# A two-layer recurrence on one core: layer 0's third state tile goes through TensorE in bfloat16 parts, and TensorE's loop body is cut at another place

## The reference

```python
def layer(x, h0, Wx, Wh, b):
    xW = jnp.einsum('ntd,dh->nth', x, Wx) + b
    def step(h_prev, xw_t):
        h_next = jnp.tanh(h_prev @ Wh + xw_t)
        return (h_next, h_next)
    _, hs = jax.lax.scan(step, h0, jnp.swapaxes(xW, 0, 1))
    return jnp.swapaxes(hs, 0, 1)
x = x + layer(x, cond, Wx0, Wh0, b0)
x = x + layer(x, cond, Wx1, Wh1, b1)
```

## Time and profile before

| | us |
|---|---|
| median of the runs | 2057.52 |
| the profiled execution's own time | 2059.2 |
| its span | 2057.4 |
| TensorE busy (matmul) | 2046.2 (99%) |
| VectorE busy | 1837.9 (89%) |
| ScalarE busy | 1539.9 (75%) |
| GpSimd busy | 444.0 (22%) |

### The profile page before, as it was taken

One profiled execution on the slowest core, in us unless ns is written; L12 is line 12 of the kernel. 1 busy time (PEld: TensorE's weight loads), 2 busy tenths in 40 slices (PEclk: granted clock), 3 DMA queues, 4 the chain that ended last, 5 costly groups with the idle time before them and its releaser, 6 DMA issues.

```text
span 2057.4 us, 224159 instructions
## 1 busy us (share of the span) xinstructions
PE 2046.2 (99%) x98384; PEld 1952.7 (95%) x98384; DVE 1837.9 (89%) x12254; ACT 1539.9 (75%) x7426; POOL 444.0 (22%) x2054
## 2 busy tenths in 40 slices
PE   8999999999999999999999999999999999999999
PEld 7999999999999999999999999999999999999998
DVE  5999999999999999999999999999999999999997
ACT  5777777777777777777777777777777777777776
POOL 3222222222222222222222222222222222222221
PEclk9999999999999999999999999999999999999999
DMA  3000000000000000000000000000000000000000
GB/s 106 28 24 28 24 27 25 26 25 26 26 25 26 25 27 24 28 24 28 24 28 24 28 24 28 24 28 24 28 24 28 24 28 24 28 24 27 25 26 18
DMA packets 111995, 56.59 MB, mean 28 GB/s; under 512 B 12432, under 2 KB 111008, under 8 KB 111520
## 3 DMA queue, kind: packets, MB, share of 16 engines
q1 hardware_dynamic: 111168, 53.53, 9.0%
q10 hardware_dynamic: 576, 1.18, 0.2%
q0 software_dynamic: 32, 0.02, 0.0%
HBM read 37.90 MB, written 16.78 MB: 27 GB/s over the span
## 4 chain that ended last, share of the span: by engine, by line
PE 99%; DMA 1%; issue 0%; DVE 0%; ACT 0%; ACTq 0%; SPq 0%
PE ps_rec L303 44%; PE ps_rec L324 33%; PE ps_xw L279 22%; DMA wx<-wx_in 0%; DMA wh<-wh_in 0%; PE ps_rec L376 0%; DVE zt L541 0%; ACT h L445 0%; SPq L255 0%; ACTq L498 0%; ACTq L497 0%; DVE x_out L581 0%; DVE z L550 0%; SPq L254 0%
## 5 line engine op out<-in xcount | busy, mean ns | idle before, releaser
L303 PE MATMUL ps_rec<-wh,h 128*32 128x128 f32 x33024 | 1271.8, 273 | 4.1 <-ACT h L445 2.7
L445 ACT ACTIVATE h<-z 128x16 f32<-128x16 f32 x4066 | 709.2, 217 | 481.7 <-DVE z L550 475.4
L324 PE MATMUL ps_rec<-wh_part,h 128*32 128x128 bf16 x48792 | 1047.4, 219 | 1.5 <-issue 1.5
L303 PEld LDWEIGHTS ps_rec<-wh,h 128*32 128x32 f32 x33024 | 832.5, 109 | 79.6 <-ACT h L445 9.2
L324 PEld LDWEIGHTS ps_rec<-wh_part,h 128*32 128x32 bf16 x48792 | 890.1, 97 | 15.4 <-issue 1.9
L541 DVE STREAM_TRANSPOSE zt<-ps_rec 128x64 f32<-128x64 f32 x4096 | 778.8, 228 | 94.0 <-PE ps_rec L303 14.2
L214 POOL TENSOR_TENSOR h<-h 128x16 f32<-128x16 f32 x2032 | 430.1, 212 | 1589.4 <-DVE h L214 1589.4
L434 ACT ACTIVATE ps_rec<-xw,mask 128x128 f32<-128x128 f32 x2040 | 731.9, 359 | 9.5 <-issue 1.0
L550 DVE TENSOR_REDUCE z<-zt 128x16 f32<-128x48 f32 x4066 | 650.6, 199 | 0.9
L214 DVE TENSOR_TENSOR h<-h 128x16 f32<-128x16 f32 x2034 | 357.3, 176 | 110.7 <-ACT h L445 2.8
L279 PE MATMUL ps_xw<-wx,x_pe 128*32 128x128 f32 x8248 | 409.9, 273 | 0.5 <-issue 0.5
(11 more groups left out here) (23 smaller groups left out, 22.3 us busy)
## 6 DMA issues: line engine op xcount, KB each, us to landing
x_pe<-x_t SPq DMA_DIRECT2D x256, 64.0 KB, 1.9
x_dve<-x_t SPq DMA_DIRECT2D x256, 64.0 KB, 2.0
out_t<-x_out SPq DMA_DIRECT2D x256, 64.0 KB, 1.7
wh<-wh_in SPq DMA_DIRECT2D x1, 1024.0 KB, 5.2
wx<-wx_in SPq DMA_DIRECT2D x1, 1024.0 KB, 8.2
wx<-wx_in ACTq DMA_DIRECT2D x1, 512.0 KB, 5.0
wx<-wx_in SPq DMA_DIRECT2D x1, 512.0 KB, 4.8
wh<-wh_in SPq DMA_DIRECT2D x1, 512.0 KB, 7.9
```

The source lines that it names most:

```text
L303: mm = pe.matmul(rows(ps_rec[l][n % 2], g), h_step(l, n - 1)[:, k, :], wh[l][:, k, g * P:(g + 1) * P], start=False, stop=k == KC - 1 and n ...
L324: mm = pe.matmul(ps_rec[l][n % 2][32 * g:32 * g + 32, cols], h_bits(l, n - 1)[:, k, :], wh_part[l][:, i, to + cols.start:to + cols.stop], ...
L445: act.activation(h_of(l, n)[:, tiles, :], src[:, tiles, :], ACT.Tanh).then_inc(h_count(l, n)[0], 1)
```

## The change

1. `KB = (3, 2)` and the table `PART_COLS`: layer 0's tile 2 goes in parts too. Its whole tiles are now only tile 3, its parts 36 matmuls and no longer 24.
2. The rests are dealt out anew. VectorE makes for layer 0 the first rest of tiles 0 and 1, then the first rest of tile 2 (which waits for the second tanh), then the second rest of tiles 0 and 1. GpSimd makes the second rest of layer 0's tile 2, and both rests of layer 1. The VectorE order of a slot has layer 0's three rests between `sum_out` and layer 1's `turn`.
3. Projected tiles go two at a time, both behind layer 0's parts; the one that stood between layer 1's parts and layer 0's whole tiles is gone from there.
4. TensorE's slot is cut in `head` (layer 0's parts, projection) and `tail` (layer 1, layer 0's next whole tiles), and the loop body begins with `tail`. All pieces of the weights, now five sets, are awaited ahead of the loop.
5. ScalarE's copies and seeds stand at other places of its slot. Where tile 2's pieces lie in other blocks (every fourth step) layer 0's second reduction runs over four blocks of 8 in place of three.

```diff
-KB = (2, 2)
+KB = (3, 2)
+PART_COLS = ((P, P, P, 0), (P, P, 0, 0))
-PROJECT = (((0, 3), (1, 0)), ((1, 1), (1, 2)), ((1, 3), (0, 0)), ((0, 1), (0, 2)))
+PROJECT = ((0, (2, 3)), (1, (0, 1)), (1, (2, 3)), (0, (0, 1)))
-BLOCKS = ((0, 1, 2), (1, 0, 2), (2, 1, 3), (3, 1, 2))
-LOWEST = (0, 0, 1, 1)
+BLOCKS = ((0, 1, 2), (1, 0, 2), (2, 0, 1), (3, 1, 2))
+LOWEST = (0, 0, 0, 1)
...
+            def head(s):
                 if s < T:
                     recur_parts(0, s)
...
+                projection(s)
+            def tail(s):
                 if (n := number(1, s)) is not None:
                     recur_whole(1, n)
                     recur_parts(1, n)
...
-                projection(s, 1)
-                if s < T:
+                if s + 1 < T:
                     recur_whole(0, s + 1)
...
-            for s in range(PARTED):
-                slot(s)
-            pe.wait_ge(s_wpart[0], PARTS * KB[0])
+            for s in range(PARTED - 1):
+                head(s)
+                tail(s)
+            head(PARTED - 1)
+            pe.wait_ge(s_wh1, DMA)
+            for l in LAYERS:
+                pe.wait_ge(s_wpart[l], PARTS * KB[l])
             with pe.Fori(0, (T - PARTED) // RING, 1):
-                for s in range(PARTED, PARTED + RING):
-                    slot(s)
+                for s in range(PARTED - 1, PARTED - 1 + RING):
+                    tail(s)
+                    head(s + 1)
...
         def _(pool):
-            for l, k in POOL_MAKES:
+            for l, k in ((0, 0), (0, 1), (1, 0), (1, 1), (0, 2)):
...
             for l, n in ORDER:
                 if is_split(l, n):
-                    pool.wait_ge(rest_done[l], n + 1 if l else n + 2 - PARTED)
-                    rest(pool, l, n, 2, HALVES[0]).then_inc(split_count(l, n, 0)[0], 1 + first)
+                    mine, done = (rest_done[1], n + 1) if l else (late_done, n + 2 - PARTED)
+                    tiles = HALVES[0] if l else slice(2, 3)
+                    if l:
+                        pool.wait_ge(*h_count(l, n, 0))
+                        rest(pool, l, n, 1, tiles).then_inc(mine, 1)
+                    pool.wait_ge(mine, done)
+                    rest(pool, l, n, 2, tiles).then_inc(split_count(l, n, 1 - l)[0], PAIR if (l, n) == (0, PARTED - 1) else 1)
...
-            def rest_first(l, n):
-                if is_split(l, n):
-                    dve.wait_ge(*h_count(l, n, 0))
-                    rest(dve, l, n, 1, HALVES[0]).then_inc(rest_done[l], 1)
+            def rests(n):
+                if is_split(0, n):
+                    dve.wait_ge(*h_count(0, n, 0))
+                    rest(dve, 0, n, 1).then_inc(rest_done[0], 1)
+                    dve.wait_ge(*h_count(0, n, 1))
+                    rest(dve, 0, n, 1, slice(2, 3)).then_inc(late_done, 1)
+                    dve.wait_ge(rest_done[0], n + 2 - PARTED)
+                    rest(dve, 0, n, 2).then_inc(split_count(0, n, 0)[0], PAIR if n == PARTED - 1 else 1)
```

More of the change, by code:

```diff
@@ L294, in recur_whole @@
                     pe.wait_ge(begun[0], 1)
-                tiles = range(in_parts(l, n), KC)
+                tiles = [k for k in range(KC) if in_parts(l, n, k) < P]
                 for k in tiles:
+                    cols = slice(in_parts(l, n, k), P)
                     if (l, n) == (0, 0):
@@ L302, in recur_whole @@
                     for g in range(QG):
-                        mm = pe.matmul(rows(ps_rec[l][n % 2], g), h_step(l, n - 1)[:, k, :],
-                                       wh[l][:, k, g * P:(g + 1) * P], start=False,
-                                       stop=k == KC - 1 and not in_parts(l, n), skip_group_check=True,
+                        out, state = rows(ps_rec[l][n % 2], g)[:, cols], h_step(l, n - 1)[:, k, :]
+                        if cols.start:
+                            out, state = out[0:B, :], h_of(l, n - 1)[:, k, :]
@@ L306, in recur_whole @@
+                        mm = pe.matmul(out, state, wh[l][:, k, g * P:(g + 1) * P][:, cols], start=False,
+                                       stop=k == KC - 1 and is_whole(l, n), skip_group_check=True,
                                        tile_position=(0, 32 * g))
-                if not in_parts(l, n):
-                    mm.then_inc(rec_done[l], 2)
+                if is_whole(l, n):
+                    mm.then_inc(rec_done[l], 1)
             def recur_parts(l, n):
-                if not in_parts(l, n):
+                if is_whole(l, n):
@@ L464, in slot @@
                     copy(1, r - 1)
+                if t == 2 and 2 <= (c := r + 2) < NG + 2:
+                    if c < NG:
+                        act.wait_ge(x_pe_loaded, DMA * (c - 1))
+                    act.wait_ge(proj_done[0], c)
+                    if c == 2:
+                        act.wait_ge(begun[0], S4)
+                        seed(0, c).then_inc(s_seed, 1)
+                    else:
+                        act.wait_ge(copied[0], copy_count(0, min(c, NG) - 1))
+                        seed(0, c).then_inc(seed0_done, 1)
                 if (n := number(1, s + 1)) is not None:
```

152 lines of the change are left out of this document (54 added, 98 removed).

## The result

The changed kernel takes 2055.11 us (median of 20 runs, 2052.93 to 2055.99); the kernel before, run between them on the same chips, 2058.26 (20 runs, 2056.92 to 2059.13). The ratio is 0.9984, its 95% interval 0.9977 to 0.999: 3.2 us or 0.16% less, less than the 0.2% that the prediction took for the least it can tell from no change, though the interval lies wholly under 1. 19 us less were forecast.

What follows compares the result with a forecast made beforehand. Layer 0's round through its rests was to replace TensorE's work as the bound: slot 1.96 for 1.98 gives -20.3 us over 1016 slots, start +1.6, median 2039 us (-0.9%); range 2024 to 2066.

Steps and rivals of the forecast that it cites:

- the forecast's own case: Whole kernel: slots of 1.945 to 1.974 us, a time of 2023 to 2053 us, chance 0.66.
- Layer 0's round through its rests: Layer 0, transposes to parts: second rest starts at 0.99, parts at 1.23, making the slot 1.96 us.
- TensorE's own work: TensorE's matmuls in a slot: 1.93 us needed, 0.05 less than before.
- The failed step: Layer 0's second reduction, every fourth step: 64 elements cost 0.016 us more than 48, or 0.004 a slot.
- 0.23 + 1.23 + 0.50: Layer 0's slot: parts' end to transposes 0.23, transposes to next parts 1.23, parts 0.50; together 1.96 us.
- The start: Before the loop: GpSimd's fifth weight set, ready at 25.2, delays layer 1's first whole tiles; +1.6 us.
- A: Rival on TensorE: it stays the bound, slot 1.93, total 2008 us; chance 0.06.
- B: Rival on layer 0's second rest: starts late, at 1.02, slot 2.00, +20 us; chance 0.18 together with C.
- C: Rival on VectorE: GpSimd's rests block reductions too, slot 2.06, total 2140 us; chance 0.04.
- D: Rival on layer 0's rests: they start between forecast and B, slot 1.975 to 1.985, 2054 to 2062 us; chance 0.10.
- A hole ahead of layer 1's whole tiles, ended by tanh: TensorE before layer 1's whole tiles: a wait of 0.02 us expected in the profile.
- free, but with nothing left at the long end: Layer 1's two GpSimd rests: matmul possible at 1.29 to 1.39, parts due at 1.385 at the earliest; no cost.

Runs made afterwards that it cites:

- e5: Changed kernel with layer 0's second reduction over three blocks in every step, and the second rest of layer 0's tiles 0 and 1 back on GpSimd: 2119.29 us.
- e1: Changed kernel with layer 0's second reduction over three blocks in every step, where every fourth had four: 2041.82 us, ratio 0.9919 to the kernel before.
- e7: e1 with two more VectorE instructions a slot that only raise and lower a semaphore, behind layer 0's rests: 2050.51 us.
- e6: e1 with layer 0's tile 2 whole as before, without its rests and its set of weight pieces: 2059.05 us.
- e3: e1 with VectorE making the second rest of layer 0's tiles 0 and 1 ahead of tile 2's first rest: 2060.72 us.
- e9: e1 with both rests of layer 0's tile 2 on GpSimd, so VectorE has one rest less: 2059.93 us.
- e8: Changed kernel with layer 0's second reduction over two blocks in every step, leaving out one piece of the sum: 2042.31 us.

## Why the prediction was wrong, and where it was right

It had the direction and the mechanism, and a gain of 19 us where 3.2 were measured. The time lies in the stated range of 2024 to 2066, but outside the forecast's own case, 2023 to 2053.

**What bounds the slot: right.** Layer 0's round through its rests. Three of four slots measure 1.955 (forecast 1.96), the second rest starts 0.99 behind the transposes (0.99), the parts 1.21 to 1.22 (1.23). e5 showed the link by making it longer: 0.08 on the link, 0.08 on the slot. TensorE's own work was forecast as 1.93, and its stretches without a hole add up to 1.930, so that 0.025 a slot are a hole, as forecast.

**The failed step** is the sentence "Every fourth step has the longer second reduction (64 elements and not 48, at about 1 ns each 0.016), which shifts tile 2's rest, and with it the second rest, in one slot of four: 0.004 a slot." The place and the path are as it says. The term is mis-sized: the reduction of 64 elements takes 0.267 and not 0.225, the slot is 0.055 longer and not 0.016, 0.0138 a slot and not 0.004. That is 10 us more than the term allowed. With it taken out, e1 measured 2041.82, against a forecast of 2039. The term was named and then not carried into the sum: 0.23 + 1.23 + 0.50 is 1.96 without it. The 1 ns for an element was taken from nothing but the shape; the trace of before had reductions of one width only, 199 ns on the mean, and no bound from both sides was set on the 64. The step should have had a far end: a reduction half as long again would have added 0.10 in one slot of four, 25 us, and with it the sum would have reached from a gain of 19 to a small loss.

**A term that was not there: the single long slots.** Before, TensorE was the bound and layer 0's round to its parts had slack, so that most of a hold-up of VectorE's was hidden, 3.0 us in all. Now VectorE lies on the link that sets the slot, and they count, up to 0.30 in one slot and 8.7 us in all. These 5.7 us are in no step of the prediction. Two things make them up, as the held places of e7's section show. VectorE itself was held 5.9 us before and 8.8 now, having 15.75 instructions a slot and not 14.25; and of the 5.9 the slots that they fall in ran 1.6 over, of the 8.8 they ran 6.7 over. In e6, with TensorE the bound again and 14.25 instructions, it is 2.7 of 6.1.

**The start: wrong by 1.6.** The fifth set was ready at 24.53, not 25.2, and what TensorE waited for it was swallowed within four slots.

**The sum, once more.** Forecast -20.3 + 1.6 = -18.7; measured in the spans -5.4. The 13.3 between them: three slots' length is 1.955 and not 1.96, -5 over all slots; the longer reduction +13.9, of which the forecast's sum had none; single long slots +5.7; start -1.6. That makes 13.0.

**Rivals.** A is out: parts wait in every slot. B is out for three slots of four: e3 put the second rest first in the queue, and it started 0.006 earlier and ended no earlier. In the fourth slot B's sign is there, a second rest at 1.048 and a slot of 2.01, and the wait is B's, in the queue behind tile 2's rest; what makes it is the longer reduction, which B didn't have. C is out: no reduction has grown under GpSimd's rests of layer 1 (first and second half 189 and 208 ns, before 189 and 209); the two-input rest in e9 has. D, a cancellation, is where the time came out, but not by its mechanism: it asked for rests that come late in every slot. (Its slots of up to 1.985 would make 2064 and not 2062.)

**What was expected of the page.** A hole ahead of layer 1's whole tiles, ended by tanh, is not there: their load waits for tanh but is 0.035 ahead of its matmul. GpSimd's rests are three a slot and end no wait of TensorE's matmuls in the changed kernel, as said; they do end the wait of layer 1's loads. The prediction let these rests end at 1.22 to 1.32 and called them "free, but with nothing left at the long end". They came out at that end, 1.33, and in e8 TensorE waits for them.

## What to carry to other kernels

When a change takes the slack out of a loop, list every instruction of the new critical link, in each of its forms, and price a form that the old trace doesn't have with a low and a high end, however small its share: here one reduction of four had a fourth block, and it took 13.3 of 16.3 us. Ask also what the old slack had been hiding; a hold-up that cost nothing when another engine was the bound comes back, here for the most part. Here the fourth block held no piece of the sum, and the version without it, e1, is the fastest of all: 2041.82 us, 0.8% less than before.

## What the runs showed of the hardware

- A reduction's time doesn't follow its elements: 187, 209 (189 in the first half) and 267 to 269 ns for 32, 48 and 64 elements a partition. The fourth block costs 58 ns; why is open.
- VectorE, in a program written out, is stopped now and then with nothing awaited, for 0.28 us in the slot shown, and most often at one and the same place in each 128 of its instructions; what the slots lose by it goes from 9.7 to 17.9 us with two more instructions a slot.
- A VectorE rest with two inputs that starts 0.03 behind a GpSimd rest takes 0.195 us and not 0.174, and ends 0.027 behind GpSimd's (e9).
- A TensorE that waits 0.025 us in every slot of 1.955 still reads 99% busy, and its matmuls show no idle time. Its weight loads show it: they start 0.002 ahead of the matmul and not 0.108, and their idle time goes from 15.4 to 181.4 us, of which a part is waiting that costs the matmuls nothing.
- The start isn't the same in all traces, of which there is one for each program: slot 12 of layer 0 begins at 35.5 to 38.9 us in these traces (36.6 in both the changed kernel and before, 38.9 in e1, whose first stages are the changed kernel's). What sets it wasn't tried. It accounts for 2.3 us of e1's profiled execution, which took 2042.9 where its fastest run took 2039.96.
